# A six-stage graph kernel on one core: more constant products in TensorE's filling and emptying steps

## The chip, the cores and the metric

One core of one Trainium2 chip runs the whole program. The time is device microseconds of that core from launch to end; three runs of the kernel before gave 923.79, 925.32 and 926.22 us. The engines are TensorE (PE), VectorE (DVE), ScalarE (ACT), GpSimd (POOL) and SyncE (SP), which issues all the transfers here. They run each its own list of instructions in order and wait for each other by semaphores.

## What is computed

128 graphs of 64 nodes with 256 features go through four layers, each with a residual and a layer normalisation behind it: two hypergraph convolutions with a hidden width of 512, a degree-weighted softmax over nodes, an eight-head attention whose scores are scaled by the adjacency matrix, and a gated layer whose attention is a product of sigmoids. Cut to what matters:

```
x = layernorm(x + L0(x, adj))   # two hypergraph convolutions, relu and layer norm between
x = layernorm(x + L1(x, adj))   # softmax over nodes of q . (adj @ k), times v
x = layernorm(x + L2(x, adj))   # 8 heads: softmax(q k^T * scale * 2 adj) v, output projection
x = layernorm(x + L3(x, adj))   # xg = x * gate; QK = sigmoid(xg Wqk^T + b)
                                # attn = rows of (QK QK^T * adj), normalised
                                # relu(attn xg Wl^T + bl + xg Wr^T)
```

## The kernel before

The 8192 tokens are cut into 32 groups of 256 (two tiles of 128 tokens, four graphs). A group's work is split into six stages, which the code calls streams 0 to 5; stage k of a group runs k steps after its stage 0. So 37 steps in all: six filling steps (the head) in which stages join one by one, 26 steps of the steady state with all six stages on six different groups (a hardware loop), and five emptying steps (the tail) in which only the last stages of the last groups are left. Values are carried as a high and a low half-precision part, so most products are three: high with high, high with low, low with high (mm3, lines 544 to 546).

Each engine has its own written-out order. A stage is a generator that stops at each yield, and a row of numbers says which stage goes on next: `ORDER_PE` for a steady step, `HEAD_PE` and `TAIL_PE` for the filling and emptying steps, and likewise for the other engines. Stages 0 to 5 are the numbers 0 to 5, and 6 is the preparation of the weights. The number 7, in TensorE's head and tail alone, is `keep_warm` (line 835): one burst of eight products of 128 rows, columns and moving columns, of a constant buffer with itself (line 848), into a PSUM bank that is free in that step. Nobody reads the result. In each step the first burst waits for a signal that the bank is free; after that the bursts wait for nothing.

```
while True:
    for _ in range(8):
        pe.matmul(bank_free[:, 0:P], same16[:], same16[:], start=True, stop=True)
    yield
```

Names that the prediction uses, with their lines in TensorE's and the other engines' lists. In the head: the column sums of the first convolution (lines 669 to 673) wait for sums on GpSimd; their result goes to VectorE's rmean; then come the products with W2 (lines 544 to 546, `bank<-W,rFh`), whose result VectorE turns into y (line 1228). HBl (line 1061) is the low part of the next group's scaled incidence matrix, on VectorE ahead of y. In the tail: Wqk3 (`bank<-xgT,Wqk`) is the first product of stage 5 on the transposed xgT, which a transposing transfer brings (line 423); ScalarE makes qt of it (line 1036) and then Qh; VectorE makes Ql, and in its order the parts of the next group's attention output follow (rinv, cxs), which another transposing transfer brings into cxT (line 430); attn_out (Wo) waits for that. The Wl products (`bank<-Wl,xgT`) wait for qt, the products of line 807 for Ql and y3l, the transposition of line 813 for the scaled attention, and the Wr products and line 830 finish a group.

Of the kernel before, what the change touches and what calls it, by code (L numbers as in the profile page):

```python
# [50 lines left out]
ORDER_DVE = [0, 2, 0, 2, 0, 1, 4, 0, 0, 0, 3, 2, 2, 3, 0, 0, 4, 0, 1, 1, 5, 1, 0, 5, 2, 3, 4, 0, 5, 4, 5, 3, 4, 5, 3, 3, 4, 1, 3, 5, 2, 1, 4, 3, 5, 5, 1, 3, 0, 5, 4, 0, 2, 0, 1, 4]  # L51
ORDER_POOL = [0, 1, 0, 1, 0, 3, 0, 1, 1, 1, 2, 2, 4, 5, 3, 1, 3, 0, 0, 0, 0, 4, 4, 5, 5, 0, 5, 0]

HEAD_PE = [[7, 7, 7, 7, 7, 7, 7, 7, 0, 7, 7, 0, 6, 0, 6, 0, 0, 6, 7, 7, 7, 7, 7, 7, 7, 0, 0], [1, 0, 7, 7, 0, 7, 0, 1, 0, 0, 7, 6, 7, 7, 1, 7, 7, 1, 0, 0, 1], [1, 2, 7, 7, 7, 2, 2, 1, 0, 2, 0, 7, 0, 7, 7, 0, 0, 1, 2, 7, 7, 1, 2, 1, 0, 0], [2, 3, 2, 1, 0, 2, 3, 0, 2, 0, 1, 0, 0, 3, 3, 7, 7, 1, 2, 7, 1, 2, 1, 0, 0], [1, 3, 2, 3, 0, 2, 1, 2, 4, 0, 2, 0, 4, 3, 3, 1, 0, 0, 2, 7, 4, 1, 2, 1, 0, 0], [3, 1, 2, 4, 3, 2, 5, 1, 4, 0, 5, 2, 0, 2, 0, 5, 3, 1, 0, 0, 3, 1, 2, 5, 4, 5, 5, 1, 2, 0, 0]]
HEAD_ACT = [[6, 0, 0, 0, 0, 6, 0, 0, 0, 0, 0, 0], [0, 6, 6, 6, 6, 0, 1, 0, 0, 0, 0, 0, 0, 0, 1, 0, 1, 1], [6, 1, 2, 0, 0, 0, 0, 2, 1, 2, 0, 0, 0, 1, 0, 0, 2, 0, 1, 2], [6, 6, 2, 0, 3, 0, 3, 0, 1, 0, 2, 6, 2, 0, 0, 0, 1, 0, 0, 1, 3, 0, 2, 3, 1, 3, 3, 2], [6, 0, 3, 1, 3, 2, 4, 0, 0, 4, 0, 1, 2, 4, 1, 4, 2, 0, 0, 0, 0, 0, 0, 2, 4, 1, 3, 3, 2, 4, 3, 4, 3], [1, 3, 4, 5, 2, 0, 5, 0, 5, 0, 3, 4, 1, 0, 2, 4, 1, 2, 0, 0, 0, 0, 0, 0, 5, 3, 1, 2, 4, 4, 3, 3, 4, 2, 3, 4, 5]]
HEAD_DVE = [[0, 0, 0, 0, 0, 0, 6, 0, 0, 0, 6, 6, 0, 6, 0, 6, 6, 6, 6, 6, 6, 0, 0, 0], [0, 0, 0, 0, 0, 0, 1, 0, 0, 0, 6, 0, 0, 1, 1, 1, 6, 1, 6, 6, 1, 0, 0, 0, 6, 1, 1], [6, 0, 1, 0, 0, 2, 2, 0, 0, 2, 0, 2, 1, 0, 0, 0, 1, 1, 0, 2, 0, 1, 2, 6, 1, 1, 2, 0, 0, 0, 1], [6, 0, 2, 0, 0, 2, 0, 0, 0, 6, 0, 0, 2, 2, 0, 3, 1, 0, 3, 2, 3, 0, 1, 1, 1, 3, 3, 3, 3, 1, 2, 1, 3, 3, 2, 0, 0, 1, 0, 1], [6, 0, 0, 0, 0, 0, 1, 2, 0, 2, 3, 0, 6, 0, 0, 1, 2, 1, 2, 4, 1, 4, 0, 3, 3, 2, 0, 4, 4, 3, 4, 4, 3, 3, 3, 1, 4, 2, 1, 3, 2, 0, 4, 1, 0, 0, 4, 3, 1], [1, 0, 2, 4, 0, 2, 0, 0, 3, 0, 0, 1, 1, 0, 0, 1, 0, 4, 2, 2, 4, 5, 0, 4, 5, 2, 4, 0, 3, 3, 5, 4, 5, 3, 5, 1, 3, 3, 5, 3, 4, 1, 2, 5, 5, 1, 5, 3, 0, 4, 2, 0, 3, 0, 4, 1]]
HEAD_POOL = [[0, 0, 0, 6, 6, 0, 0, 0, 0, 0, 0, 0], [0, 6, 0, 0, 0, 1, 1, 1, 1, 1, 0, 0, 0, 0, 1, 0, 0], [6, 1, 0, 1, 0, 0, 0, 1, 1, 1, 1, 6, 2, 2, 0, 0, 0, 0, 0, 0], [0, 0, 0, 0, 3, 1, 1, 2, 2, 1, 1, 1, 1, 0, 3, 3, 0, 0, 0, 0, 0], [0, 0, 1, 0, 1, 0, 4, 1, 1, 1, 3, 2, 2, 3, 1, 3, 0, 0, 0, 4, 0, 4, 0, 0], [1, 3, 1, 0, 0, 0, 0, 1, 1, 1, 4, 1, 2, 2, 5, 3, 0, 0, 0, 3, 4, 0, 4, 5, 5, 0, 5, 0]]
TAIL_PE = [[3, 1, 2, 4, 4, 3, 5, 1, 2, 2, 5, 2, 5, 3, 3, 5, 4, 1, 2, 5, 5, 1, 2, 7, 7, 1], [3, 2, 4, 3, 5, 4, 2, 2, 5, 2, 5, 7, 3, 3, 5, 4, 2, 5, 5, 2], [3, 7, 4, 7, 7, 4, 3, 5, 7, 5, 7, 7, 5, 4, 5, 3, 3, 5, 5], [7, 7, 7, 7, 7, 7, 7, 7, 7, 7, 7, 5, 4, 7, 4, 5, 7, 7, 5, 7, 7, 5, 4, 5, 5], [7, 7, 7, 7, 7, 7, 7, 7, 7, 7, 7, 7, 5, 7, 5, 7, 7, 5, 7, 7, 5, 5, 5]]
TAIL_ACT = [[3, 1, 4, 4, 4, 3, 5, 2, 5, 5, 2, 1, 5, 2, 4, 1, 4, 2, 3, 3, 4, 3, 4, 1, 2, 3, 5], [3, 4, 3, 5, 2, 5, 4, 4, 4, 5, 2, 2, 5, 3, 2, 3, 4, 3, 3, 4, 2, 4, 5], [3, 4, 4, 4, 3, 5, 5, 5, 4, 5, 4, 4, 3, 4, 3, 3, 3, 5], [5, 5, 4, 4, 4, 5, 5, 4, 4, 4, 4, 5], [5, 5, 5, 5, 5]]
TAIL_DVE = [[1, 2, 4, 4, 2, 4, 3, 4, 4, 3, 1, 3, 4, 2, 1, 2, 5, 1, 5, 2, 5, 5, 5, 3, 3, 5, 3, 4, 3, 1, 2, 5, 3, 4, 5, 4, 5, 1, 2, 1, 3, 1], [4, 3, 2, 2, 3, 2, 4, 4, 4, 4, 2, 4, 3, 5, 5, 2, 5, 5, 5, 3, 3, 3, 5, 3, 4, 2, 3, 5, 5, 3, 5, 4, 2, 4], [4, 3, 4, 4, 4, 4, 3, 4, 5, 3, 5, 5, 5, 5, 4, 5, 3, 3, 3, 5, 4, 3, 4, 3, 5, 5, 3], [4, 4, 5, 4, 4, 4, 4, 5, 5, 5, 5, 5, 4, 5, 4, 5, 4, 5], [5, 5, 5, 5, 5, 5, 5, 5, 5]]  # L60
TAIL_POOL = [[1, 1, 3, 4, 1, 1, 1, 5, 2, 2, 3, 1, 3, 4, 4, 5, 5, 5], [3, 4, 2, 5, 2, 3, 3, 4, 4, 5, 5, 5], [4, 5, 3, 4, 4, 3, 3, 5, 5, 5], [4, 5, 4, 4, 5, 5, 5], [5, 5, 5, 5]]
# [8 lines left out]
def build(nc, x, adj_bd, adj_tile, adj_graph, adj_mask, w1t, b1, gamma, beta, w2t, b2, wqk1t, wv1, wqt, bq, wkt, bk, wvt, bv,  # L70
          wot, bo, wqk3t, bqk, wlt, bl, wrt, wd, bd, out):
    ctx = ExitStack()
    with ctx:
# [225 lines left out]
        def run(eng, order, head, tail, streams, set_up, early=0):  # L299

            pieces = set_up()

            def step(j, s, lo, hi, order):
                live = {k: streams[k](At(k, j, s)) for k in range(lo, hi + 1)}
                if j is None and s <= LAST_LAG:
                    live[SETUP] = pieces
                if j is None and len(streams) > SETUP:
                    live[WARM] = streams[SETUP](s)
                for k in order:
                    next(live[k], None)  # L310
                live.pop(SETUP, None)
                live.pop(WARM, None)
                assert all(next(live[k], "end") == "end" for k in live)

            first = LAST_LAG + 1
            last = first + (GROUPS - first) // 2 * 2
            for s in range(first):
                step(None, s, 0, s, head[s])
            assert next(pieces, "end") == "end"
            with eng.Fori(first // 2, (last - early) // 2) as j:  # L320
                for par in range(2):
                    step(j, par, 0, LAST_LAG, order)
            for s in range(last - early, last):
                step(None, s, 0, LAST_LAG, order)
            for s in range(last, STEPS):
                step(None, s, max(0, s - GROUPS + 1), LAST_LAG, tail[s - last])
# [214 lines left out]
        def _(pe):  # L541
# [308 lines left out]

            run(pe, ORDER_PE, HEAD_PE, TAIL_PE, [stream0, stream1, stream2, stream3, stream4, stream5, keep_warm], set_up)

# [738 lines left out]
```

How the kernel before makes its waits and increments, by code:

```python
            def load_x(at):  # L353
                if at.earlier(2):
                    sp.wait_ge(ev("preB"), at.n(-2)).then_inc(ev("sp_held"), 1)
                sp.dma_start(xin[:, at.par], at_group(xv, at)).then_inc(ev(f"x_in{at.par}"), 16)
# [1 line left out]
            def load_conv(at):  # L358
                if at.earlier(2):
                    sp.wait_ge(ev("h_t"), at.n(-2)).then_inc(ev("sp_held"), 1)
                    sp.wait_ge(ev("w_lo"), at.chain(3, 3, -2)).then_inc(ev("sp_held"), 1)
                sp.dma_start(atA[:, at.par], at_group(adj_bd, at)).then_inc(ev(f"at_in{at.par}"), 16)
# [1 line left out]
            def load_layer1(at):  # L364
                if at.earlier(2):
                    sp.wait_ge(ev("adj_masked"), at.n(-2)).then_inc(ev("sp_held"), 1)
                    sp.wait_ge(ev("w_masked"), at.n(-2)).then_inc(ev("sp_held"), 1)
                sp.dma_start(aC[:, at.par], at_group(adj_mask, at)).then_inc(ev(f"C_in{at.par}"), 16)
# [1 line left out]
            def load_layer2(at):  # L370
                if at.earlier(2):
                    sp.wait_ge(ev("s_masked"), at.tile(1, -2)).then_inc(ev("sp_held"), 1)
                    sp.wait_ge(ev("deg"), at.n(-2)).then_inc(ev("sp_held"), 1)
                sp.dma_start(acD[:, at.par], at_group(adj_tile, at)).then_inc(ev(f"acD_in{at.par}"), 16)
# [13 lines left out]
            def fetch(name, dram, dst, parts, at):  # L388
                sp.wait_ge(ev(name + "_parked"), at.chain(16, 16)).then_inc(ev("sp_held"), 1)
                for r, hl in enumerate(parts):
```

## Time and profile before

| | |
|---|---|
| median of 3 runs | 925.32 us (923.79 to 926.22) |
| the profiled execution's own time | 924.93 us |
| its span, first to last instruction | 923.1 us |
| TensorE busy | 869.6 us, 94% |
| VectorE, ScalarE, GpSimd busy | 754.2, 714.0 and 638.7 us |
| constant products (line 848) | 632, 42.6 us busy |
| mean granted TensorE clock | 0.993 of full |

The span starts at the first instruction that is counted, so the own time is 1.8 us longer. Busy time of TensorE contains the constant products. The granted clock is the share of the full 2.4 GHz that the chip lets TensorE have; only 1.0 and 0.5 occur, a value between is a mean over a stretch that has both. Times inside the execution are us from the span's start. The length shown for one matmul includes its way through the array, so neighbours overlap; the distance from start to start says how fast they go. A wait's end is named behind the arrow.

### The profile page before, as it was taken

The page shows a single profiled execution, that of the slowest core. Times are in us where ns is not written, and L with a number is a line of the kernel's source. Part 1 is how long each engine was busy: PE and PEld are TensorE (multiplying, and loading weights), DVE is VectorE, ACT ScalarE, POOL GpSimd, SP SyncE. Part 2 cuts the span into 40 slices and gives each one's busy share as a digit, 9 for nine tenths or more (in the row PEclk, how much of TensorE's full clock was granted, in tenths as well). Part 3 has the DMA queues.
Part 4 walks back from the last instruction along what each step waited for, and adds up shares of the span by engine and source line. Part 5 has one row for each costly group of instructions (what it writes and reads, how often), then busy time and mean ns, then how long its engine had stood idle before and what let it go on. Part 6 is the DMA issues. An engine that isn't in the chain of part 4 may idle for free.

```text
span 923.1 us, 35018 instructions
## 1 busy us (share of the span) xinstructions
PE 869.6 (94%) x12500; PEld 754.3 (82%) x12500; DVE 754.2 (82%) x2356; ACT 714.0 (77%) x1740; POOL 638.7 (69%) x973
## 2 busy tenths in 40 slices
PE   7788899999999999999999999999999999988884
PEld 7667787888888888888888888888888888877773
DVE  6567888888888899888888888988888888887651
ACT  4457777888888888889888888888888888876541
POOL 2667766777778777778777877777777777764321
PEclk9999999999999999999999999999999999999998
DMA  7003556555555665555555555555555555565521
GB/s 223 24 25 90 139 115 164 138 121 132 132 131 142 152 154 142 142 133 132 128 131 133 140 149 154 142 145 133 132 128 133 131 141 145 137 133 122 145 61 35
DMA packets 239633, 118.40 MB, mean 128 GB/s; under 512 B 145634, under 2 KB 239332, under 8 KB 239588
## 3 DMA queue, kind: packets, MB, share of 16 engines
q1 hardware_dynamic: 239588, 117.80, 50.8%
q8 instruction: 28, 0.46, 0.2%
q14 instruction: 17, 0.14, 0.0%
HBM read 50.38 MB, written 25.17 MB: 82 GB/s over the span
## 4 chain that ended last, share of the span: by engine, by line
PE 62%; DVE 11%; ACT 10%; DMA 6%; issue 4%; SPq 4%; POOL 3%; ACTq 0%; DVEq 0%; POOLq 0%
PE bank L544 17%; PE bank L546 16%; PE bank L545 16%; PE bank L830 2%; DMA Ks<-k_by_head 2%; ACT x L888 2%; ACT x L877 2%; PE bank L777 2%; DVE x1Fl L1061 1%; PE bank L705 1%; SPq L392 1%; DVE cxs L1341 1%; PE bank L673 1%; DMA k_by_head<-kst 1%; DVE late L1312 1%
## 5 line engine op out<-in xcount | busy, mean ns | idle before, releaser
L1418 POOL TENSOR_TENSOR rFl<-r,rFh 128x512 f16<-128x512 f32 x64 | 73.1, 1162 | 15.8 <-ACT rFh L857 15.8
L1519 POOL TENSOR_TENSOR late<-late,Smx 128x512 f32<-128x512 f32 x64 | 66.8, 1045 | 16.9 <-DVE Smx L1317 16.9
L888 ACT ACTIVATE late<-preG,nbG,rsG 128x256 f32<-128x256 f32 x64 | 34.9, 592 | 52.9 <-POOL nbG L1440 52.9
L544 PE MATMUL bank<-z1h,W 128*128 128x256 f16 x256 | 70.1, 274 | 2.0 <-DVE z1l L1061 1.5
L545 PE MATMUL bank<-W,rFh 128*128 128x256 f16 x256 | 70.6, 276 | 0.0
L546 PE MATMUL bank<-W,rFl 128*128 128x256 f16 x256 | 70.5, 276 | 0.0
L544 PE MATMUL bank<-W,rFh 128*128 128x256 f16 x256 | 70.4, 275 | 0.0
L546 PE MATMUL bank<-z1h,W 128*128 128x256 f16 x256 | 69.8, 273 | 0.0
L545 PE MATMUL bank<-z1l,W 128*128 128x256 f16 x256 | 69.8, 273 | 0.0
L1061 DVE SCALAR_TENSOR_TENSOR x2Fl<-bank,x2Fh 128x512 f16<-128x512 f32 x32 | 22.1, 691 | 48.5 <-ACT x2Fh L857 48.5
L1418 POOL TENSOR_TENSOR y0l<-y,y0h 128x512 f16<-128x512 f32 x32 | 37.1, 1160 | 26.0 <-ACT y0h L857 26.0
L917 ACT ACTIVATE r<-bank,b1c 128x256 f32<-128x256 f32 x128 | 50.6, 474 | 2.8 <-PE bank L546 2.8
L1430 POOL TENSOR_SCALAR veG<-mvG 128x2 f32<-128x2 f32 x32 | 19.1, 597 | 45.3 <-DVE mvG L1166 45.3
L1323 DVE TENSOR_TENSOR Ehl<-E,Ehl 128x512 f16<-128x512 f32 x64 | 46.6, 729 | 0.5 <-ACT Ehl L857 0.5
L857 ACT ACTIVATE z1h<-bank 128x512 f16<-128x512 f32 x32 | 19.1, 598 | 35.9 <-PE bank L546 35.9
L1312 DVE TENSOR_TENSOR late<-bank,acD 128x512 f32<-128x512 f32 x64 | 43.6, 681 | 3.8 <-PE bank L761 3.8
L1445 POOL TENSOR_TENSOR gp<-late,bdb 128x512 f32<-128x512 f32 x32 | 40.8, 1276 | 7.8 <-ACT late L1005 7.8
L544 PE MATMUL bank<-Wv,x2Fh 128*128 128x128 f16 x256 | 44.8, 220 | 0.0
L848 PE MATMUL bank<-same 128*128 128x128 f16 x632 | 42.6, 226 | 2.3 <-DVE same L1078 2.3
L546 PE MATMUL bank<-Wv,x2Fl 128*128 128x128 f16 x256 | 44.5, 219 | 0.0
L545 PE MATMUL bank<-Wv,x2Fh 128*128 128x128 f16 x256 | 44.5, 219 | 0.0
L1317 DVE TENSOR_REDUCE Smx<-late 128x8 f32<-128x512 f32 x64 | 43.0, 672 | 0.2
(279 smaller groups left out, 4143.1 us busy)
## 6 DMA issues: line engine op xcount, KB each, us to landing
Qs<-q_by_head SPq DMA_DIRECT2D x96, 128.0 KB, 2.7
Ks<-k_by_head SPq DMA_DIRECT2D x96, 128.0 KB
Vbd<-vst SPq DMA_DIRECT2D x128, 66.0 KB, 2.0
xin<-x SPq DMA_DIRECT2D x32, 256.0 KB, 2.9
q_by_head<-qst SPq DMA_DIRECT2D x32, 256.0 KB, 2.3
k_by_head<-kst SPq DMA_DIRECT2D x32, 256.0 KB, 2.2
out<-late SPq DMA_DIRECT2D x32, 256.0 KB, 2.2
aC<-adj_mask SPq DMA_DIRECT2D x32, 129.0 KB, 2.1
```

The costliest lines, as they stand in the source:

```text
L544: pe.matmul(o, sh, mh, start=start, stop=False, skip_group_check=True)
L545: pe.matmul(o, sh, ml, start=False, stop=False, skip_group_check=True)
L546: return pe.matmul(o, sl, mh, start=False, stop=stop, skip_group_check=True)
L848: pe.matmul(bank_free[:, 0:P], same16[:], same16[:], start=True, stop=True)
L888: m = act.activation(dst[:, t], pre[k][:, t], ACT.Identity, bias=nb[k][:, t:t + 1], scale=rs[k][:, t:t + 1])
L917: m = act.activation(r[:, 2 * i + c], (bA, bB)[i][:, c * TOK:(c + 1) * TOK], ACT.Relu, bias=b1c[:, 2 * i + c:2 * i + c + 1], scale=1.0 / WS)
L1312: dve.tensor_tensor(Sm[:, t], (bD0, bD1)[t][:].rearrange("p (h k) -> p h k", h=HEADS), acD[:, at.par, t:t + 1].broadcast_to([P, HEADS, NOD ...
L1317: dve.tensor_reduce(Smx[:, t], Sm[:, t], AX.X, ALU.max).then_inc(ev("s_max"), 1)
L1323: dve.tensor_tensor(Ehl[:, t, 1], E[:, t], Ehl[:, t, 0], ALU.subtract).then_inc(ev("e_lo"), 1)
L1418: return pool.tensor_tensor(dst, a, b, ALU.subtract)
L1445: return pool.tensor_tensor(dst, src, b[:].rearrange("p (o d) -> p o d", o=1).broadcast_to([P, TILES, D]), ALU.add)
L1519: pool.tensor_tensor(Ssb[:, t], Sm[:, t], Smx[:, t:t + 1].rearrange("p t h -> p h t").broadcast_to([P, HEADS, NODES]), ALU.subtract).then_ ...
```

## The change

Two tables of numbers: more 7s in `HEAD_PE` and `TAIL_PE`. Counted in the tables, the head has 57 bursts in place of 37 and the tail 71 in place of 42, together 128 in place of 79, 1024 products in place of 632. All other numbers stand in the same sequence, and the other engines' tables are untouched. The diff, of which the tail's table is shown:

```diff
@@ -51,11 +51,11 @@
...
-TAIL_PE = [[3, 1, 2, 4, 4, 3, 5, 1, 2, 2, 5, 2, 5, 3, 3, 5, 4, 1, 2, 5, 5, 1, 2, 7, 7, 1], [3, 2, 4, 3, 5, 4, 2, 2, 5, 2, 5, 7, 3, 3, 5, 4, 2, 5, 5, 2], [3, 7, 4, 7, 7, 4, 3, 5, 7, 5, 7, 7, 5, 4, 5, 3, 3, 5, 5], [7, 7, 7, 7, 7, 7, 7, 7, 7, 7, 7, 5, 4, 7, 4, 5, 7, 7, 5, 7, 7, 5, 4, 5, 5], [7, 7, 7, 7, 7, 7, 7, 7, 7, 7, 7, 7, 5, 7, 5, 7, 7, 5, 7, 7, 5, 5, 5]]
+TAIL_PE = [[3, 1, 2, 4, 4, 3, 5, 1, 2, 2, 5, 2, 5, 3, 3, 5, 4, 1, 2, 5, 5, 1, 2, 7, 7, 7, 7, 1], [3, 2, 4, 3, 5, 4, 2, 2, 5, 2, 5, 7, 7, 3, 3, 5, 4, 2, 5, 5, 2], [3, 7, 4, 7, 7, 7, 4, 3, 5, 7, 7, 5, 7, 7, 7, 5, 4, 5, 3, 3, 5, 5], [7, 7, 7, 7, 7, 7, 7, 7, 7, 7, 7, 7, 7, 7, 7, 7, 7, 7, 5, 4, 7, 4, 5, 7, 7, 7, 5, 7, 7, 7, 7, 5, 4, 5, 5], [7, 7, 7, 7, 7, 7, 7, 7, 7, 7, 7, 7, 7, 7, 7, 7, 7, 7, 7, 7, 5, 7, 7, 5, 7, 7, 7, 5, 7, 7, 7, 7, 5, 7, 5, 5]]
...
```

Three places in TensorE's list, as pieces of the difference. In a piece, `[waits x]` is the semaphore that the instruction waits for, and a minus or plus the row before and after the change.

The first step of the head. L606 is a product of the preparation of the weights, L669 the first of the column sums.

```order
 L606 MATMUL bank<-late 128x256 [waits second_in]
 L606 MATMUL bank<-late 128x256 x3
-L848 MATMUL bank<-same 128x128 x56
+L848 MATMUL bank<-same 128x128 x88
 L669 MATMUL bank<-ones,rFh 128x1 [waits sq_sum,relu,rF_lo1,rF_lo0]
 L671 MATMUL bank<-ones,rFl 128x1
```

Four bursts more stand ahead of the sums; nothing else moved.

The fourth step of the tail: ahead of the Wqk3 products of the group before the last.

```order
 L830 MATMUL bank<-y3h,SAl 64x256 x2
 L848 MATMUL bank<-same 128x128 [waits r_mean]
-L848 MATMUL bank<-same 128x128 x87
+L848 MATMUL bank<-same 128x128 x143
 L544 MATMUL bank<-xgT,Wqk 128x256 [waits xg_turned]
 L545 MATMUL bank<-xgT,Wqk 128x256
```

Seven bursts more, 88 products become 144. In the fifth step the piece is the same with 96 and 160.

The end of the fifth step: the last group's attention.

```order
 L807 MATMUL bank<-Ql,Qh 64x64 x2
 L807 MATMUL bank<-Qh,Ql 64x64 x2
-L848 MATMUL bank<-same 128x128 x16
+L848 MATMUL bank<-same 128x128 x32
 L813 MATMUL bank<-ident,SAs 128x128 [waits attn_scaled]
+L848 MATMUL bank<-same 128x128 x8
 L820 MATMUL bank<-blr,ones 128x512 [waits attn_lo]
```

Two bursts more stand ahead of the transposition, and there is a new burst behind it.

## Rows read from the trace of the kernel before

**Rows 1.** The page, busy time and the granted clock in 40 equal slices.

```profile
PE 869.6 (94%) x12500; PEld 754.3 (82%) x12500; DVE 754.2 (82%) x2356; ACT 714.0 (77%) x1740; POOL 638.7 (69%) x973
...
PEclk9999999999999999999999999999999999999998
```

**Rows 2.** Windows: busy us of each engine (instructions), PEclk, DMA share, GB/s.

```profile
27.00:30.50 3.50, 3.50 (x19) 2.51 (x18) 2.81 (x8) 0.57 (x2) 3.15 (x7) 0.51 0.00 0
...
904.25:907.65 3.40, 3.32 (x21) 2.41 (x20) 0.69 (x1) 1.47 (x3) 0.00 (x0) 0.50 0.01 4
...
907.65:917.90 10.25, 5.93 (x88) 4.54 (x86) 3.47 (x13) 0.87 (x2) 0.67 (x3) 1.00 0.00 0
...
917.90:923.10 5.20, 0.00 (x0) 0.00 (x0) 0.00 (x0) 1.09 (x2) 1.12 (x3) 0.50 0.15 50
```

**Rows 3.** Timeline of TensorE, head: start, us, instruction, [idle before <-what ended it].

```profile
20.84 3.29 PE L848 MATMUL bank<-same 128*128 128x128 f16 x56
...
25.41 0.16 PE L669 MATMUL bank<-ones,rFh 128*128 128x1 f16 x1 [1.27 <-POOL rsq L1476]
...
30.38 0.32 PE L546 MATMUL bank<-W,rFl 128*128 128x256 f16 x1
```

**Rows 4.** Timeline of TensorE, tail, the last group's Wqk3 and Wl products.

```profile
895.58 5.53 PE L848 MATMUL bank<-same 128*128 128x128 f16 x96
...
903.29 0.28 PE L544 MATMUL bank<-xgT,Wqk 128*128 128x256 f16 x1 [2.18 <-DMA xgT<-xgs]
...
904.28 0.41 PE L544 MATMUL bank<-xgT,Wqk 128*128 128x256 f16 x1
...
904.92 1.06 PE L848 MATMUL bank<-same 128*128 128x128 f16 x8
...
906.05 0.39 PE L544 MATMUL bank<-Wl,xgT 128*128 128x256 f16 x1
...
908.15 1.06 PE L848 MATMUL bank<-same 128*128 128x128 f16 x16
```

**Rows 5.** Timeline of TensorE, the tightest of the covered places.

```profile
50.31 1.50 PE L848 MATMUL bank<-same 128*128 128x128 f16 x24
52.55 0.30 PE L716 MATMUL bank<-ident,wrm 128*128 128x128 f32 x1 [0.74 <-DVE wrm L1268]
```

**Rows 6.** Timeline of VectorE, head.

```profile
26.43 0.16 DVE L1213 TENSOR_SCALAR rmean<-bank 128x2 f32<-128x2 f32 x1 [0.56 <-PE bank L673]
...
29.37 0.61 DVE L1061 SCALAR_TENSOR_TENSOR HBl<-HT,be,HBh 128x128 f16<-128x128 f16 x2
...
30.74 0.87 DVE L1228 SCALAR_TENSOR_TENSOR y<-bank,rsc,c 128x256 f32<-128x256 f32 x2 [0.75 <-PE bank L546]
```

**Rows 7.** Timeline of TensorE, tail, near 835 us.

```profile
835.54 1.06 PE L848 MATMUL bank<-same 128*128 128x128 f16 x16
837.17 0.22 PE L705 MATMUL bank<-x1Fh,uh 128*64 128x64 f16 x2 [0.57 <-DVE ul L1061]
```

**Rows 8.** Timeline of TensorE, tail, the burst of 88.

```profile
875.39 5.09 PE L848 MATMUL bank<-same 128*128 128x128 f16 x88
...
882.06 0.28 PE L544 MATMUL bank<-xgT,Wqk 128*128 128x256 f16 x1 [1.59 <-DMA xgT<-xgs]
...
883.50 0.57 PE L777 MATMUL bank<-Vbd,PT 128*64 128x66 f16 x24
```

**Rows 9.** The chain that ended last: start us, us, what.

```profile
883.72 0.73 ACT qt L1036 x2
...
887.45 4.37 DMA cxT<-cxs
```

**Rows 10.** Timeline of TensorE, the last transposition.

```profile
910.23 1.07 PE L848 MATMUL bank<-same 128*128 128x128 f16 x16
911.86 0.33 PE L813 MATMUL bank<-ident,SAs 128*128 128x128 f32 x1 [0.56 <-POOL SAs L1535]
```

**Rows 11.** Tile xgT: landings of its transfer.

```profile
DMA to landing us min/median/max: 3.1/3.2/4.1
```

More of the change, by code:

```diff
@@ L52 @@
 ORDER_POOL = [0, 1, 0, 1, 0, 3, 0, 1, 1, 1, 2, 2, 4, 5, 3, 1, 3, 0, 0, 0, 0, 4, 4, 5, 5, 0, 5, 0]
-HEAD_PE = [[7, 7, 7, 7, 7, 7, 7, 7, 0, 7, 7, 0, 6, 0, 6, 0, 0, 6, 7, 7, 7, 7, 7, 7, 7, 0, 0], [1, 0, 7, 7, 0, 7, 0, 1, 0, 0, 7, 6, 7, 7, 1, 7, 7, 1, 0, 0, 1], [1, 2, 7, 7, 7, 2, 2, 1, 0, 2, 0, 7, 0, 7, 7, 0, 0, 1, 2, 7, 7, 1, 2, 1, 0, 0], [2, 3, 2, 1, 0, 2, 3, 0, 2, 0, 1, 0, 0, 3, 3, 7, 7, 1, 2, 7, 1, 2, 1, 0, 0], [1, 3, 2, 3, 0, 2, 1, 2, 4, 0, 2, 0, 4, 3, 3, 1, 0, 0, 2, 7, 4, 1, 2, 1, 0, 0], [3, 1, 2, 4, 3, 2, 5, 1, 4, 0, 5, 2, 0, 2, 0, 5, 3, 1, 0, 0, 3, 1, 2, 5, 4, 5, 5, 1, 2, 0, 0]]
+HEAD_PE = [[7, 7, 7, 7, 7, 7, 7, 7, 0, 7, 7, 7, 0, 6, 0, 6, 0, 0, 6, 7, 7, 7, 7, 7, 7, 7, 7, 7, 7, 7, 0, 0], [1, 0, 7, 7, 7, 0, 7, 7, 0, 1, 0, 0, 7, 6, 7, 7, 7, 7, 1, 7, 7, 7, 1, 0, 0, 1], [1, 2, 7, 7, 7, 7, 7, 2, 2, 1, 0, 2, 0, 7, 7, 0, 7, 7, 7, 0, 0, 1, 2, 7, 7, 7, 7, 1, 2, 1, 0, 0], [2, 3, 2, 1, 0, 2, 3, 0, 2, 0, 1, 0, 0, 3, 3, 7, 7, 7, 7, 1, 2, 7, 7, 1, 2, 1, 0, 0], [1, 3, 2, 3, 0, 2, 1, 2, 4, 0, 2, 0, 4, 3, 3, 1, 0, 0, 2, 7, 7, 4, 1, 2, 1, 0, 0], [3, 1, 2, 4, 3, 2, 5, 1, 4, 0, 5, 2, 0, 2, 0, 5, 3, 1, 0, 0, 3, 1, 2, 5, 4, 5, 5, 1, 2, 0, 0]]
 HEAD_ACT = [[6, 0, 0, 0, 0, 6, 0, 0, 0, 0, 0, 0], [0, 6, 6, 6, 6, 0, 1, 0, 0, 0, 0, 0, 0, 0, 1, 0, 1, 1], [6, 1, 2, 0, 0, 0, 0, 2, 1, 2, 0, 0, 0, 1, 0, 0, 2, 0, 1, 2], [6, 6, 2, 0, 3, 0, 3, 0, 1, 0, 2, 6, 2, 0, 0, 0, 1, 0, 0, 1, 3, 0, 2, 3, 1, 3, 3, 2], [6, 0, 3, 1, 3, 2, 4, 0, 0, 4, 0, 1, 2, 4, 1, 4, 2, 0, 0, 0, 0, 0, 0, 2, 4, 1, 3, 3, 2, 4, 3, 4, 3], [1, 3, 4, 5, 2, 0, 5, 0, 5, 0, 3, 4, 1, 0, 2, 4, 1, 2, 0, 0, 0, 0, 0, 0, 5, 3, 1, 2, 4, 4, 3, 3, 4, 2, 3, 4, 5]]
```

## The prediction

> **What bounds the kernel now.** I read the page first: TensorE is busy 94% of the span, and the row of its granted clock stands at 9 (90% or more) until the last of 40 slices [rows 1]. The busy share contains the constant products, so it is not all real work, and a mean can't say where a product costs something. What matters is the end of each wait: TensorE takes its instructions in order, so a constant product ahead of a waiting one costs nothing as long as the burst is done before the awaited signal comes, and its full length after that.
>
> Second, the windows: the granted clock is 1.00 nearly everywhere, but 0.50 (the lower level, 1.2 GHz, in place of 2.4) in two stretches of about 3.4 us, one at 27.0 to 30.4 us and one at 904.25 to 907.65 us; behind the second it reads 1.00 again [rows 2]. I call them the two dips. What TensorE did before each: it stood idle for 1.27 us after the burst of 56 products [rows 3], and for 2.18 us after the burst of 96 [rows 4]. A third, after 917.9 us, lies where TensorE has no work left [rows 2], and costs nothing.
>
> Third, the chain of waits: in the last 50 us it alternates between short pieces on each engine and transposing transfers, and TensorE's pieces of the last two steps are on it. There a delay moves the end.
>
> **The measure.** 96 products took 5.53 us and 56 took 3.29 us [rows 3, 4]: 2.24 us for 40, or 0.056 us each at the upper level; a burst of eight is 0.45 us. The free time of a place is the start of the instruction after the burst, less the burst's start, less its number times 0.056 us. The change adds products at 25 of the 29 places and opens one new place: 632 products become 1024, 49 bursts of eight more. Nothing is removed or moved, and the lists of the other four engines and of the DMA queue are the same, so no wait is new.
>
> **The places that are covered.** At 19 of the 26 places the added 0.45 or 0.90 us fit into the free time. At two more, near 109.7 and 888.6 us, they run over by less than a burst of eight, and TensorE has a longer wait for another engine or a transfer before its next result is needed. The tightest is at 50.31 us: 24 products end at 51.65, the transpose behind them starts at 52.55, which leaves 0.90 us for 16 more, 0.90 us [rows 5]. I cost all of them at nothing; what hides them is the wait of TensorE for a vector or scalar result, and if that result came earlier, each place would cost at most its own 0.45 or 0.90 us. The five others follow.
>
> **Head, the place of 56, now 88.** Free: 25.41 - 20.84 - 56 x 0.056 = 1.43 us [rows 3]. Added: 32 x 0.056 = 1.79. So the column sums start 0.36 us later, and with them VectorE's chain from rmean on (26.43), which runs without a gap to the end of HBl at 29.98 and so ends at 30.34 [rows 6]. In return the gap of 1.27 us before the sums is gone, and I expect the clock to stay up. The W2 products ran at half speed until 30.4 us; at full speed they are done near 29.4 (30.7, less half of 3.4, plus 0.36), so y on VectorE, which waited 0.75 us for them until 30.74 [rows 6], can start when HBl ends, at 30.34. What is late next is VectorE itself. Gain: **-0.40 us**. The bound on the good side is the whole dip, 3.4 us at half speed, or 1.7 us, less the 0.36; on the bad side the dip stays and the 0.36 is paid. I take the one between, since VectorE's row says so.
>
> **Tail, 835.54 us.** 16 products become 32; free 837.17 - 835.54 - 0.90 = 0.73, added 0.90: **+0.17 us** [rows 7]. Behind it TensorE has no gap up to the qk3 result that ScalarE waits for, so I charge it; the other bound is nothing.
>
> **Tail, 875.39 us, 88 products become 144.** Free: 882.06 - 875.39 - 88 x 0.056 = 1.74 us. Added: 56 x 0.056 = 3.14. The Wqk3 products of the group before the last start 1.40 us late [rows 8]. Who waits: ScalarE's qt. It started at 883.72 on the chain [rows 9], about 0.1 us after the twelve products were done (the next group starts at 883.50 [rows 8]), so 0.1 of the 1.40 is covered. Behind qt come Qh, then Ql on VectorE, and behind Ql in VectorE's order rinv and the product for cxs, and so the transfer into cxT at 887.45 [rows 9], for which attn_out and everything up to the next big burst wait. **+1.30 us.**
>
> **Tail, 895.58 us, 96 products become 160.** It starts behind those products, so it shifts with them, and its own free time stays: 903.29 - 895.58 - 96 x 0.056 = 2.33 us. Added: 64 x 0.056 = 3.58. **+1.25 us** on the last group's Wqk3 products, which are on the chain [rows 4].
>
> **The second dip.** With 160 products there is no gap before them. I expect the clock to stay up through them. In the trace three of the twelve Wqk3 products run at half speed, 904.28 to 904.92, 0.64 us in place of 0.33; and the Wl products from 906.05 to 908.15 take 2.10 us [rows 4] in place of 12 x 0.11 = 1.32. Together 0.31 + 0.78, about **-1.10 us**. The added eight between the two groups then end before qt does.
>
> **Tail, 910.23 us, 16 become 32.** Free 911.86 - 910.23 - 0.90 = 0.73, added 0.90: **+0.17 us** on the last transposition, whose result the end waits for [rows 10]. The new burst of eight behind it fits into the wait for the low part.
>
> **Sum.** -0.40 + 0.17 + 1.30 + 1.25 - 1.10 + 0.17 = +1.39 us against the profiled execution's own 924.93 us: **926.3 us**. That execution is 0.39 us below the median of the three runs, 925.32, which is well inside their spread of 2.4 us; I don't correct for it. Against the median it is 0.1% more, and a measurement of this kernel can tell 0.3% from no change, that is below 922.5 or above 928.1 us.
>
> **Rivals.**
>
> *The dips stay, and the overruns are paid: slower.* The mechanism is the same order of TensorE, its place are the two big bursts of the tail, and it decides at the Wqk3 products of the last group: if the clock reads 0.50 in the 3.4 us around them or behind them, nothing pays for the bursts. Head +0.36 in place of -0.40; tail 0 in place of -1.10, and the added eight products between the last group's Wqk3 and Wl now run at half speed: 16 x 0.11 = 1.76 us from 904.92, but only 1.13 are free, so +0.6. Sum 0.36 + 0.17 + 1.30 + 1.25 + 0.6 + 0.17 = +3.85: **928.8 us**. For it: idle gaps as long as these stand in other places of the trace without a dip behind them (1.59 us before 882.06 [rows 8]), so the gap alone doesn't decide. Against it: both dips do follow the largest gaps of their neighbourhood. If only the tail's dip stays it is 928.0, if only the head's, 927.1.
>
> The Trainium skill (TensorE: Matmul & The Clock Gate, section Why this matters for your kernels) advises against idle gaps between bursts of matmuls, but only against gaps longer than any of these. By that rule the dips are not the gaps' doing and filling them gives nothing back, which is this rival. The trace speaks against it, since the level fell behind gaps of 1.27 and 2.18 us [rows 2, 3, 4].
>
> *The overruns aren't paid: 923.4 us.* If the transposed data land later than in this execution, the longer bursts are covered. Landings of this transfer span 3.1 to 4.1 us [rows 11], and the one before 903.29 already took 3.8; so at most 0.3 of the 1.25 is covered that way, and only a cause that I don't see hides the whole. Then -0.40 - 1.10 = -1.50. If the head also got its full bound (-1.34 in place of -0.40), 922.5 us: the only way to a measurable gain.
>
> **Chances.** Forecast 0.52. Both dips stay or others appear, 928.8: 0.15. One dip stays, 927.1 to 928.0: 0.16. Overruns mostly unpaid, 923.4: 0.11. The full credit, 922.5 or less: 0.06. Faster by over 0.3%: 0.06; slower by over 0.3%: 0.16, the first rival and a little of the third line; within 0.3%: 0.78. The range takes in the bounds of the overruns and of the dips: 923.4 to 928.8.
>
> **What would show it.** In the new profile: the clock's rows without 0.50 before about 917 us; no idle time between the bursts of 88, 144 and 160 and what follows them; y starting 0.4 us earlier; the last group's Wqk3 products 2.3 us later (-0.40 + 0.17 + 1.30 + 1.25), its Wl products in 1.3 us; everything between 130 and 835 us only shifted. Idle time left before the Wqk3 products would refute the overruns; a reading of 0.50 there would refute the term of -1.10.

## The result and the profile after

| | before | after |
|---|---|---|
| median of 20 runs each, side by side | 925.36 us (922.33 to 930.18) | 928.94 us (926.59 to 931.38) |
| ratio of the two, 95% interval | | 1.0036 [1.0026, 1.0046] |
| the profiled execution's own time | 924.93 | 928.98 |
| its span | 923.1 | 927.2 |
| TensorE busy | 869.6 us, 94% | 888.0 us, 96% |
| mean granted clock | 0.993 | 0.997 |

The change makes the kernel slower by 0.36%, or 3.3 us. Applied to the 925.32 us of the prediction this is 928.7 us: inside the range (923.4 to 928.8), at its upper end, 2.4 us above the forecast of 926.3, and on the side of the first rival. From the ratios of the experiments below two executions are left out, one of before with 1000.0 us and one of e3 with 997.6 us, both at a granted clock of 0.85.

The page of after, to be read against [rows 1]:

```profile
PE 888.0 (96%) x12892; PEld 774.9 (84%) x12892; DVE 755.4 (81%) x2356; ACT 713.1 (77%) x1740; POOL 639.8 (69%) x973
...
PEclk9999999999999999999999999999999999999999
...
q8 instruction: 31, 0.51, 0.2%
```

The other engines do what they did. The third line is from the list of DMA queues; its counterpart before is in no row of the prediction:

```profile
q8 instruction: 28, 0.46, 0.2%
```

I take that queue to carry program code: 28 packets before, 31 after. 392 more products are 784 more instructions, since each counts once as weight load and once as matmul, so three packets more is about one for every 256. The other kernels go the same way: 29 packets with 32 to 120 products more than before, 30 with 160, 31 from 272 on.

**The places that the sum was made of.** TensorE's timeline of after, head and tail; columns as in [rows 3] and [rows 4]:

```profile
21.03 5.08 PE L848 MATMUL bank<-same 128*128 128x128 f16 x88
25.95 0.17 PE L669 MATMUL bank<-ones,rFh 128*128 128x1 f16 x1
...
834.44 1.95 PE L848 MATMUL bank<-same 128*128 128x128 f16 x32
...
843.93 0.57 PE L777 MATMUL bank<-Vbd,PT 128*64 128x66 f16 x24 [1.15 <-DMA PT<-Ehl]
...
877.98 8.21 PE L848 MATMUL bank<-same 128*128 128x128 f16 x144
886.03 0.27 PE L544 MATMUL bank<-xgT,Wqk 128*128 128x256 f16 x1
...
899.42 9.11 PE L848 MATMUL bank<-same 128*128 128x128 f16 x160
908.37 0.27 PE L544 MATMUL bank<-xgT,Wqk 128*128 128x256 f16 x1
...
910.77 0.28 PE L544 MATMUL bank<-Wl,xgT 128*128 128x256 f16 x1
...
912.09 1.50 PE L848 MATMUL bank<-same 128*128 128x128 f16 x24
```

Nothing stands idle any more behind the bursts of 88, 144 and 160, and the last group's Wl products take 1.32 us (910.77 to 912.09) where they took 2.10. The clock in the two places of [rows 2], and where it is low now:

```profile
27.00:30.50 3.50, 2.58 (x24) 2.05 (x22) 3.26 (x12) 1.09 (x3) 2.60 (x7) 1.00 0.00 0
845.70:849.10 3.40, 3.40 (x18) 2.35 (x16) 3.12 (x9) 1.89 (x4) 0.00 (x0) 0.50 0.50 154
908.37:912.10 3.73, 3.69 (x44) 3.25 (x42) 0.69 (x1) 1.47 (x3) 0.00 (x0) 1.00 0.02 4
```

Both dips went, as expected, and one came where TensorE works without a gap: 3.40 us busy of 3.40. The prediction had asked for no 0.50 before about 917 us, so this sign speaks against it.

Starts of six landmarks and the own time in the two profiled executions, and how far after is behind, beside what the sum of the prediction makes of it:

| landmark | before | after | behind | forecast |
|---|---|---|---|---|
| burst near 835 us | 835.54 | 834.44 | -1.10 | -0.40 |
| burst of 88, now 144 | 875.39 | 877.98 | **+2.59** | -0.23 |
| its Wqk3 products | 882.06 | 886.03 | +3.97 | +1.17 |
| burst of 96, now 160 | 895.58 | 899.42 | +3.84 | +1.07 |
| its Wqk3 products | 903.29 | 908.37 | +5.08 | +2.32 |
| burst behind the Wl products | 908.15 | 912.09 | +3.94 | +1.22 |
| own time | 924.93 | 928.98 | +4.05 | +1.39 |

From the second landmark on, the steps between the lines are the forecast's to 0.06 us. The miss lies between the first and the second: +3.69 us where +0.17 was expected. The 0.70 us that after is further ahead at the first landmark take part of it back, and they aren't clearly the change's: e12_before_copy, a repeat of the kernel before, gains 0.8 us on before's trace in the same place, between 820 and 835 us. Behind the burst near 835 us TensorE's list has four small additions in this stretch, eight products each, of the kind that the prediction costed at nothing.

### The profile page after: what moved, and what is told of

Same layout as the page of the kernel before. It is cut to its first block, busy times and chain, and to the rows that moved or that the text cites. A ratio compares the mean times of both kernels' runs of the same rounds, so it can differ in the third digit from the quotient of the medians.

```text
span 927.2 us, 35802 instructions
## 1 busy us (share of the span) xinstructions
PE 888.0 (96%) x12892; PEld 774.9 (84%) x12892; DVE 755.4 (81%) x2356; ACT 713.1 (77%) x1740; POOL 639.8 (69%) x973
## 4 chain that ended last, share of the span: by engine, by line
PE 65%; DVE 11%; ACT 9%; DMA 7%; issue 4%; POOL 3%; SPq 2%; ACTq 0%; POOLq 0%; DVEq 0%
PE bank L544 17%; PE bank L546 15%; PE bank L545 15%; PE bank L848 4%; PE bank L830 2%; ACT x L877 2%; ACT x L888 2%; DMA Ks<-k_by_head 2%; DMA k_by_head<-kst 2%; DVE x1Fl L1061 2%; PE bank L705 2%; DVE Smx L1317 1%; DVE cxs L1341 1%; PE bank L673 1%; DVE late L1312 1%
## 5 line engine op out<-in xcount | busy, mean ns | idle before, releaser
L848 PE MATMUL bank<-same 128*128 128x128 f16 x1024 | 63.8, 222 | 2.3 <-DVE same L1078 2.3
L848 PEld LDWEIGHTS bank<-same 128*128 128x128 f16 x1024 | 60.5, 99 | 3.5 <-POOL ident L1405 2.3
```

## Where the 3.69 us come from

Three things in that stretch differ. First, an instruction of VectorE. The timelines of GpSimd and VectorE, of before:

```profile
837.92 1.07 POOL L1440 TENSOR_SCALAR nbG<-mvG,rsG 128x1 f32<-128x1 f32 x2 [0.21 <-POOL rsG L1434]
...
838.13 0.72 DVE L1323 TENSOR_TENSOR Ehl<-E,Ehl 128x512 f16<-128x512 f32 x1
...
838.95 1.27 POOL L1445 TENSOR_TENSOR x2b<-x,bob 128x512 f32<-128x512 f32 x1
```

and of after:

```profile
836.79 0.51 POOL L1440 TENSOR_SCALAR nbG<-mvG,rsG 128x1 f32<-128x1 f32 x2 [0.21 <-POOL rsG L1434]
...
837.26 1.81 DVE L1323 TENSOR_TENSOR Ehl<-E,Ehl 128x512 f16<-128x512 f32 x1
...
837.26 1.27 POOL L1445 TENSOR_TENSOR x2b<-x,bob 128x512 f32<-128x512 f32 x1
```

Ehl takes 1.81 us in place of 0.72. Before, it began 0.21 us behind GpSimd's nbG, GpSimd's pair took 1.07 us and x2b began 0.10 us after Ehl was done; now it begins 0.47 us behind nbG, the pair takes 0.51, x2b begins in the same hundredth as Ehl, and VectorE is the one that takes long. TensorE's column products (L705) had started 0.2 us later behind the longer burst, and VectorE's wscr, which stands ahead of Ehl and needs them, now waits for them. The Trainium skill (SBUF — State Buffer, section Who interferes with whom) says that a VectorE instruction with two SBUF inputs contends with a GpSimd instruction that reads SBUF, that the ports the two engines share are an exclusive lock, and that the order of issue decides who is blocked. The trace agrees: either engine pays, 0.56 us on GpSimd before and 1.09 us on VectorE after.

Second, the transfer behind Ehl. The DMA views of just these stretches (queue: packets, MB, share; and the transfer with its us to landing), of before:

```profile
PT<-Ehl SPq DMA_TRANSPOSE x1, 3.2
```

and of after:

```profile
q8 instruction: 1, 0.02, 2.0%
...
PT<-Ehl SPq DMA_TRANSPOSE x1, 4.7
```

A packet of code starts 1.1 us into the transfer of after; in before one starts 3.0 us into it, 0.25 us ahead of the landing. TensorE waits for PT at 843.93, above.

Third, the dip at 845.7 us, above.

## The experiments

Twelve kernels, in three groups of four. In the diffs `7 x11` stands for eleven 7s in the table. The kernel before ran beside them, 29 to 35 times in each group, with medians of 925.32, 926.27 and 925.99 us; each ratio is against that of its own group, and differences in us below are worked out from the ratios where nothing else is said. The ratio isn't exactly that of the two medians.

### Are the two big bursts the cost?

The first theory was the prediction's: the overruns are the loss, the dips the gain. Label e1_big_only has nothing but the two big bursts.

```diff
-TAIL_PE[3] = [7 x11, 5, 4, ...]   TAIL_PE[4] = [7 x12, 5, 7, ...]
+TAIL_PE[3] = [7 x18, 5, 4, ...]   TAIL_PE[4] = [7 x20, 5, 7, ...]
```

> Only the two big bursts of the tail grow, 88 to 144 and 96 to 160 products; all else as before. Theory 1, the loss is the overrun of these two bursts: 1.30 + 1.25 us later, so +2.5 us (928) where the dip behind the second one is not typical of the kernel before, and +1.4 us (926.8) where it is and is filled. Rival 2, the loss comes from the many small bursts: within 0.5 us of before. In the trace both theories want 1.4 and 1.2 us more from the burst's start to the Wqk3 products than the kernel before has.

Measured: 924.92 us, ratio 0.9998 [0.9977, 1.0019]. Label e2_without_big is the change with those two places as before.

```diff
-TAIL_PE[3] = [7 x18, 5, 4, ...]   TAIL_PE[4] = [7 x20, 5, 7, ...]
+TAIL_PE[3] = [7 x11, 5, 4, ...]   TAIL_PE[4] = [7 x12, 5, 7, ...]
```

> The changed kernel with the two big bursts back at 88 and 96 products; all small ones as changed. Theory 1: no more than 1 us above before (-0.4 + 0.17 + 0.17, and up to 0.6 for a dip). Rival 2, the small bursts do it: it keeps the 3.6 us of the changed kernel. If both carry a part, 1 to 2 us.

Measured: 924.25 us, 0.9983 [0.9964, 1.0001]. Label e3_head_only has the change's `HEAD_PE` and the old `TAIL_PE`; of the head's six rows the first:

```diff
-HEAD_PE[0] = [7 x8, 0, 7 x2, 0, 6, 0, 6, 0, 0, 6, 7 x7, 0, 0]
+HEAD_PE[0] = [7 x8, 0, 7 x3, 0, 6, 0, 6, 0, 0, 6, 7 x11, 0, 0]
...
```

> Only the head's 20 added bursts. My forecast gave -0.4 us. Theory 1 with the steady state giving nothing on: 0 us, since the lead of 0.3 us that the changed kernel has at 100 us is gone at 200 us. Rival 3, the head's bursts cost where no free time is left: +0.5 to +1 us.

Measured: 921.96 us, 0.9958 [0.9939, 0.9977]: 3.9 us faster than its before (3.4 by the medians), where the prediction's term for the head was 0.40. Label e4_big_fitted sizes the two bursts to the free time.

```diff
-TAIL_PE[3] = [7 x11, 5, 4, ...]   TAIL_PE[4] = [7 x12, 5, 7, ...]
+TAIL_PE[3] = [7 x14, 5, 4, ...]   TAIL_PE[4] = [7 x16, 5, 7, ...]
```

> The two big bursts grow only as far as the free time goes: 88 to 112 (1.34 us of 1.74) and 96 to 128 (1.79 us of 2.33). No overrun. If the dip at 904 us is typical of the kernel before and comes of the gap, this one is 1.1 us faster than before; if it isn't typical, within 0.5 us of before. Against both: if the length of the burst costs something by itself and not by the wait, +1 us.

Measured: 925.52 us, 0.9997 [0.9977, 1.0017].

So neither the big bursts nor everything else makes the kernel slower by itself, and the sum of single costs doesn't hold. That theory falls as a statement on the time, although its distances are in the traces: in e1 burst to burst again takes 20.19 us with 144 products, as before with 88. The reason came out of the DMA view of the last transfer into cxT. Before, its 4.37 us [rows 9] hold a packet of code:

```profile
q8 instruction: 1, 0.02, 1.6%
...
cxT<-cxs SPq DMA_TRANSPOSE x1, 4.4
```

In e1 there is none in it, and it lands in less:

```profile
cxT<-cxs SPq DMA_TRANSPOSE x1, 2.7
```

The only other transfer beside it, the store of a group's result, is issued 1.35 us behind it in both traces. The overrun of 1.4 us had been paid for by a transfer that was 1.7 us shorter. The other overrun of 1.2 us isn't covered by it; what levels e1 besides stands below, with the clock of each execution.

### Which combination?

Label e5_after_again is the change once more, without an edit, beside its parts.

> The changed kernel itself, beside the three partial ones on one chip. Its ratio should be 1.002 to 1.005 again (+2 to +5 us). If it comes out near 1.000, the first comparison of the parts says little and everything lies within the chip's own spread.

Measured: 929.30 us, 1.0034 [1.0018, 1.0050]. Label e6_small_tail_only: old head, old big bursts, all other 7s of the tail as in the change.

```diff
-TAIL_PE[0] = [..., 1, 2, 7 x2, 1]   TAIL_PE[3] = [7 x11, 5, 4, 7, 4, 5, 7 x2, 5, 7 x2, ...]
+TAIL_PE[0] = [..., 1, 2, 7 x4, 1]   TAIL_PE[3] = [7 x11, 5, 4, 7, 4, 5, 7 x3, 5, 7 x4, ...]
...
```

> Only the tail's small bursts as changed (14 bursts at 11 places), head and both big bursts as before. Theory 1 (the big bursts' overrun is the loss): +0.3 us, two places of 0.17. From the second kernel of the first comparison, which lost 2.3 us against the one with the head alone, a rival: the small places cost +1 to +2.5 us, where the transfers land sooner than in the profiled execution of before and the places have less free time.

Measured: 925.23 us, 0.9991 [0.9970, 1.0012]. Label e7_head_and_big: the change with all small 7s of the tail as before.

```diff
-TAIL_PE[0] = [..., 1, 2, 7 x4, 1]   TAIL_PE[3] = [7 x18, 5, 4, 7, 4, 5, 7 x3, 5, 7 x4, ...]
+TAIL_PE[0] = [..., 1, 2, 7 x2, 1]   TAIL_PE[3] = [7 x18, 5, 4, 7, 4, 5, 7 x2, 5, 7 x2, ...]
...
```

> The head's bursts and both big bursts as changed, the tail's small ones as before. Theory 1, with the price as I worked it out: head -1 to -3.4 us (the head alone was 3.4 faster), big bursts +2.5, together -1 to +1.5. If the big ones cost what the changed kernel has over the one without them (4.7 us), +1.3 or more. If the big bursts cost nothing, as their own run had it, -3.4.

Measured: 924.97 us, 0.9985 [0.9966, 1.0004]. Label e8_big_doubled is e7 with the two additions made twice as long.

```diff
-TAIL_PE[3] = [7 x18, 5, 4, ...]   TAIL_PE[4] = [7 x20, 5, 7, ...]
+TAIL_PE[3] = [7 x25, 5, 4, ...]   TAIL_PE[4] = [7 x28, 5, 7, ...]
```

> As the one before, but the big bursts with twice the addition: 88 to 200 and 96 to 224 products. It adds 56 and 64 products, 3.13 + 3.58 = 6.7 us, which lie wholly on the way if the longer bursts already run over: +6.7 us against the kernel with head and big bursts. If the addition so far was covered, less by what was covered.

Measured: 934.16 us, 1.0082 [1.0053, 1.0110]: 9.2 us over e7, where 6.7 were expected. Its trace has two dips in the head, at 10.7 and 102.8 us, and the tail from the burst near 835 us to the last normalisation takes 92.69 us in place of e7's 84.91, 7.8 more for 15 bursts of 0.45, or 6.7. The rest is in the trace too: the last cxT lands in 4.3 us, with a packet of code, in place of e7's 2.7. So once the free time is used up, a longer burst costs its full length.

Against before, head alone gives -3.9 us, small tail bursts alone -0.8, big ones alone -0.2, head and small -1.6, head and big -1.4, and all three +3.2. On top of the head the small bursts cost 2.3 and the big ones 2.5, but both together 7.1, 2.3 more than the sum. The traces have 2.2 of these 2.3 us in the last cxT, which lands in 3.4 us with the head alone, in 2.7 in e2 and e7, and in 4.3 in after and e5. But each interval is about 2 us wide to either side, so the excess itself isn't clear of noise. Small and big without the head weren't tried.

The stretch in which the prediction failed is a ladder in all these traces: from the start of the burst near 835 us to the products on PT (L777), and from there to the products of line 807.

| kernels | PT lands | Ehl | to L777 | to L807 |
|---|---|---|---|---|
| before, e1, e4, e12 | 3.1 to 3.2 | 0.72 | 6.92 to 6.96 | 4.91 |
| new head or e9's: e3, e11, e8, e9 | 4.3 to 4.9 | 0.72 | 7.77 to 8.39 | 4.91 |
| e7, dip at 844.2 us | 4.6 | 0.72 | 8.14 | 5.71 |
| small tail bursts: e2, e5, e10 | 4.4 to 4.8 | 1.81 | 9.23 to 9.60 | 4.91 |
| after, dip at 845.7 us | 4.7 | 1.81 | 9.49 | 5.72 |
| e6, dip at 849.2 us | 5.1 | 1.82 | 9.91 | 5.72 |

Ehl takes 1.8 us in each of the five kernels that have the small bursts of the tail and in none of the nine without them; the late PT comes with every change here of the number of products ahead of it, and the packet then starts inside the transfer. For the profiled execution of after the table gives 1.2 us for PT, 1.3 for Ehl with what leads to it, and 0.8 for the dip, 3.3 of the 3.69. The last 0.3 us lie between the products of line 807 and the big burst and stay open; kernels with equal tables differ there by 1.6 us (e3 and e11: 27.15 and 28.78 us). In that stretch e11 has a dip, at 862.7 us, and so have e5 and e9 (28.95 and 28.69 us), while e3 has none.

### Is it where the code packets fall?

The theory by then: a packet of code in a transposing transfer makes it longer, and each burst added anywhere moves all later packets. Label e9_before_shifted tests that without the places in dispute: before, with four bursts more in the very first burst, or 64 instructions. e3 adds 320; the difference is 256, one whole packet, so behind the head the packets of both fall at the same places in the program.

```diff
-HEAD_PE[0] = [7 x8, 0, 7, 7, 0, ...]
+HEAD_PE[0] = [7 x12, 0, 7, 7, 0, ...]
```

> Theory 4: TensorE's own code is loaded in 16 KB packets, one per 256 of its instructions, and a packet that falls into a transposing transfer makes it 1.2 to 1.6 us longer; the number of constant products decides where the packets fall. This kernel is before with 32 products more in the very first burst alone (64 to 96), in 2.2 us of free time. They are 64 instructions, the same shift modulo 256 as the head's 20 bursts (320). Theory 4: in the trace the last transfer into cxT takes 3.4 or less and not 4.4 us, that into xgT 3.1 and not 3.8, and the time falls by about 2 us. Rival, the burst's clock credit or free time alone decides: the tail's landings stay at 4.4 and 3.8, and the time is within 0.5 us of before.

Measured: 923.27 us, 0.9978 [0.9956, 1.0000], 2.0 us under before by the ratio, whose interval just reaches no change, and 2.7 by the medians. In its DMA view of 901.4 to 904.6 us the last transfer into xgT is alone:

```profile
xgT<-xgs SPq DMA_TRANSPOSE x1, 3.1
```

where the same view of before, 899.4 to 903.3 us, has

```profile
q8 instruction: 1, 0.02, 2.0%
...
xgT<-xgs SPq DMA_TRANSPOSE x1, 3.8
```

The last cxT missed the expectation of 3.4 us or less: it still has a packet in it and lands in 3.6.

Label e10_after_shifted is the reverse: the change with three bursts fewer in the fourth step of the head.

```diff
-HEAD_PE[3] = [..., 7 x4, 1, 2, 7 x2, 1, 2, 1, 0, 0]
+HEAD_PE[3] = [..., 7 x2, 1, 2, 7, 1, 2, 1, 0, 0]
```

> The changed kernel without 3 of the head's added bursts (32 products back to 16 and 16 back to 8, in the fourth step), 48 instructions less ahead of the tail. Theory 4: the packet that falls into the last transfer into cxT (893.5 in 891.4 to 895.7) comes after it; the transfer takes 2.8 in place of 4.3 us and the time falls by 1 to 1.5 us against the changed kernel. Rival: the landing stays at 4.3, the time within 0.3 us of the changed kernel.

Measured: 929.21 us, 1.0031 [1.0012, 1.0049]. The last cxT lands in 2.7 us, as the theory says, the packet now falling at its very end:

```profile
q8 instruction: 1, 0.02, 3.8%
...
cxT<-cxs SPq DMA_TRANSPOSE x1, 2.7
```

and from the burst near 835 us to the last normalisation its trace takes 86.68 us, 2.25 less than the 88.93 of after. But the time isn't lower. The profiled execution had lost it in the head, where it is 2.8 us behind at 800 us, part of it in a dip that after's doesn't have:

```profile
10.10:13.50 3.40, 3.28 (x34) 3.29 (x35) 3.15 (x10) 0.63 (x2) 0.00 (x0) 0.50 0.41 103
```

So e10 shows the transfer and not the time, and the theory's forecast of 1 to 1.5 us less was missed. Labels e11_head_only_again (e3's tables) and e12_before_copy (the tables of before) are repeats without an edit, as a measure of what a comparison like this is worth.

> The kernel with the head's bursts alone once more, to see whether its 3.4 us against before hold: ratio 0.996 (0.994 to 0.998), last transfers 3.4 and 3.1 us again. If it were chance, 0.999 to 1.001.

Measured: 922.98 us, 0.9970 [0.9952, 0.9989].

> The kernel before itself, under another name: what the comparison gives for no change, ratio 1.000 within its interval. Theory 4 also says that its code packets fall into the last transfers into cxT and xgT again, with landings of 4.2 to 4.4 and 3.6 to 3.8 us; if the long landings of the first profile were chance, 2.8 and 3.1.

Measured: 927.75 us, 1.0016 [0.9998, 1.0034]: equal kernels came out 1.8 us apart by the medians, so differences of 1 to 2 us in the matrix above are no more than hints, while the change itself (1.0036, 1.0034) and its head alone (0.9958, 0.9970) stand clear of that. In e12's trace both last transfers hold their packet again and take 4.6 and 3.7 us, and the dip behind the second is there again, as in [rows 2]:

```profile
903.40:906.80 3.40, 3.32 (x21) 2.36 (x19) 0.18 (x1) 1.47 (x3) 0.00 (x0) 0.50 0.17 56
```

In e3, where xgT lands in 3.1 us, TensorE's wait is shorter and no dip follows. TensorE's timeline of e3:

```profile
842.45 0.57 PE L777 MATMUL bank<-Vbd,PT 128*64 128x66 f16 x24 [1.13 <-DMA PT<-Ehl]
...
893.74 5.53 PE L848 MATMUL bank<-same 128*128 128x128 f16 x96
...
900.77 0.28 PE L544 MATMUL bank<-xgT,Wqk 128*128 128x256 f16 x1 [1.50 <-DMA xgT<-xgs]
```

**The granted clock of each execution** is on record too, and it explains much of this scatter. Of 98 executions of the kernel before, the 28 with a mean clock of 0.991 or less have a median of 928.4 us and the 21 with 0.996 or more one of 923.2. Within the kernels, over 255 executions of all of them, 0.001 of the mean clock goes with 0.68 us; one dip of 3.4 us at half speed is 0.0018, so by this estimate 1.3 us. The means are 0.993 for before in each group, 0.997 for after and e5, 0.996 to 0.997 for e2, e3, e7 and e11, 0.995 for e1 and e9, 0.994 for e4 and e6, and 0.992 for e12. So, as estimates from these numbers, the change gives back 2.1 to 2.7 us by a higher clock; about 2 of the 3 to 4 us of the head alone come that way, 1.3 us of e1, 1.0 of e9, and 1.1 of the 1.8 us between e12 and before. The low clock behind the end of TensorE's work, 5.1 to 7.6 us in the traces, is in these means and costs nothing; by it alone two kernels can differ by 0.001.

With that the sum closes roughly: overruns of 2.5 us, 2.5 us for Ehl and PT and 0.2 at the last transposition, less 2.1 to 2.7, is 2.5 to 3.1 us, where 3.3 was measured.

**The best version found** is the head alone: faster than before in two comparisons, by 0.42% and 0.30%, and, by these ratios, 0.7% faster than the change.

## Why the prediction was right and where it was not

**What bounds the kernel, and the measure:** right. 0.056 us a product gives 144 and 160 to 0.1 us (877.98 to 886.03, 899.42 to 908.37), and in the tail each delay reached the end.

**The big bursts, +1.30 and +1.25:** right in the trace. Burst to burst takes 21.45 us in place of 20.19 (+1.26), and the second burst's start to its Wqk3 products 8.95 in place of 7.71 (+1.24). But 2.33 us of free time at the second place was not the usual: it held the 0.7 us of a code packet. In e3 the same distance gives 900.77 - 893.74 - 5.38 = 1.65 us. With a transfer as quick as e3's the overrun is 1.9.

**The second dip, -1.10:** right, the clock is 1.00 and the distance from the Wqk3 products to the end of Wl 3.72 in place of 4.86 us. The reason given, no gap and therefore no dip, was too narrow. Seven traces have the burst of 96 there. The dip comes in the two whose xgT takes 3.7 or 3.8 us, with a packet in it, and where TensorE then waits for 2.1 to 2.2 us (before, e12), and in none of the five with 3.1 us and waits of 1.4 to 1.5 us (e2, e3, e6, e9, e11). So shifting the packet does it as well.

**The head, -0.40:** right as a reading of its place: y starts at 30.45 in place of 30.74, and no dip there. None of the eight kernels with the new first step has a dip between 25 and 60 us; the six others have five between them, though e1 and e9, with the same gap of 1.26 us, have none. What it is worth was misjudged, since it was read from one dip in one execution. After's lead is gone by 200 us (within 0.2 us up to 800). Head alone is 2.8 to 3.9 us faster. About 2 us of that go with the higher clock, by the estimate above, which is the prediction's own mechanism at a larger size. In the one pair of traces the tail of e3 takes 81.39 us in place of 83.77, with 3.4 and 3.1 us for the last cxT and xgT in place of 4.4 and 3.8, and without the second dip. e9, which shares the position of the packets and not the bursts of the head, gets 2.0.

**835.54 us, +0.17, and "the places that are covered":** this is the step that failed. The prediction asked of each place whether TensorE would be late, and named as the bound of a small place "at most its own 0.45 or 0.90 us". At 835 us TensorE was late by 0.2 us and the stretch grew by 3.69. Three terms were missing: a delay far smaller than the burst turned the order of VectorE and GpSimd at Ehl (about 1.3 us), the added code moved a packet into PT (1.2 us), and a dip came in a busy stretch (0.8 us). The first two are in all four traces with head and small bursts. A dip between 844 and 866 us is in four of the eight kernels with a new head (after, e5, e7, e11) and in two of the six others (e6, e9), and whether it belongs to the change is not shown.

**The first rival** named the side and nearly the size, but not for its reason: it needed the clock at 0.50 around the last Wqk3 products, and there it is 1.00. **The range** held the time because it had been stretched to that rival, so that the number lies in it is luck in part: 2.5 us for Ehl and PT, which no term of the sum had, were set off in part by a clock that, by the estimate above, gave 2.1 to 2.7 us in place of the sum's 1.5. "Nothing is removed or moved", with the conclusion that no wait is new, was wrong twice: the order between two engines moved, and the program's own code is a load on the DMA queues.

Open are why e10, whose last cxT is 1.6 us shorter than after's, isn't faster; the last 0.3 us ahead of the burst of 88; and whether the place of a dip in a busy stretch has a cause in the kernel.

## What to carry to other kernels

Cost an added filler instruction twice: by its time at its place, and as code, which moves every later fetch; look at what the fetches fall on now before taking a wait of the profile for its usual length, best over several repetitions of the same transfer. Where two engines' instructions start within some tenths of a microsecond of each other, treat their order as something that any small delay can turn. Compare the granted clock of the executions before two times: here executions of one kernel that differ in it lie 5 us apart. And measure the parts of a change apart as well as together: here the head alone is worth 0.3 to 0.4%, and the rest gave it back.

## What the runs showed of the hardware

**Code packets and transposing transfers.** Over the fourteen profiled executions (for cxT the twelve whose traces have its landing), behind 800 us:

| transfer | no packet starts in it, median (largest) | a packet lies wholly in it, median (range) |
|---|---|---|
| cxT | 2.78 (3.17) us, 44 times | 4.27 (3.39 to 4.70), 13 times |
| PT | 3.08 (3.73), 77 times | 4.61 (3.38 to 5.06), 24 times |
| xgT | 3.11 (4.16), 48 times | 4.06 (3.23 to 4.92), 16 times |

A packet that starts near the end of a transfer needn't cost: before's PT landed in 3.2 us and e10's cxT in 2.7. The Trainium skill (Runtime: NRT & Kernel Launch, section Instruction fetch mechanics) says that code is refilled in blocks of 16 KiB, 256 instructions, and that the cost of it is mostly hidden. The count of packets agrees with the first (784 instructions, 3 packets); that a transfer on the critical path pays 0.7 to 1.7 us for one (xgT 3.8 against 3.1, cxT 4.4 against 2.7 us) speaks against the second here.

**Dips.** In these traces the clock also fell in stretches without a gap, each time to 0.50 for 3.4 us, as in after at 845.7 and in e4 three times. Windows of e4:

```profile
12.20:15.60 3.40, 3.40 (x10) 2.64 (x9) 2.33 (x7) 0.38 (x1) 0.00 (x0) 0.50 0.61 149
29.30:32.70 3.40, 3.40 (x26) 2.59 (x24) 2.88 (x9) 0.00 (x0) 3.32 (x7) 0.50 0.00 0
56.60:60.00 3.40, 3.40 (x22) 2.66 (x23) 1.91 (x8) 0.62 (x2) 0.87 (x2) 0.50 0.37 118
```

TensorE's longest waits behind 800 us bear on the dips as well. Waits of 2.07 to 2.42 us occur there six times in the fourteen traces, each for a transposing transfer that had a packet in it and took 3.7 to 5.0 us; five are followed by a dip within 1.4 us (before, e12, e5, e9, e11). The sixth, in e3, is not:

```profile
861.80 0.57 PE L777 MATMUL bank<-Vbd,PT 128*64 128x66 f16 x24 [2.41 <-DMA PT<-Ehl]
```

Of 44 gaps of 1.2 to 1.9 us behind the first 12 us of the traces, six are followed by one within 3 us. So a packet can cost twice, by the transfer and by a dip behind it, and no gap seen here brings a dip each time.

By 60 us e4 is 2.8 us behind before's trace, by which one dip or another in the head moves the time of a single execution.
